# Decoder layer on one core: one transposed copy of h, waits in another order, first tile and gate-weight sum on VectorE

## What is computed

```python
def weight_quant(w):
    scale = 1.0 / jnp.clip(jnp.mean(jnp.abs(w)), 1e-05, None)
    return jnp.clip(jnp.round(w * scale), -1, 1) / scale

def _L0_ffn_ref(x, gate_w, down_w, gate_norm_w, down_norm_w):
    y = bit_linear(x, gate_w, gate_norm_w)
    gate, up = jnp.split(y, 2, axis=-1)
    h = gate * jax.nn.sigmoid(gate) * up
    return bit_linear(h, down_w, down_norm_w)

x = x + _L0_attn_ref(_layernorm(x, axis=-1), L0_attn_W_qkv, L0_attn_W_out)
x = x + _L0_xattn_ref(_layernorm(x, axis=-1), ctx_2048, mask_BxS2_bk0)
x = x + _L0_ffn_ref(_layernorm(x, axis=-1), L0_ffn_gate_w, L0_ffn_down_w, L0_ffn_gate_norm_w, L0_ffn_down_norm_w)
```

## Time and profile before

| | us |
|---|---|
| median of 3 runs | 209.47 |
| lowest and highest | 208.86, 209.68 |
| the profiled execution | 208.5 |
| its span, first to last instruction | 206.5 |
| busy in it: PE, DVE, ACT, POOL | 186.9, 165.7, 152.2, 113.8 |

### The profile page before, as it was taken

One profiled execution on the slowest core, in us unless ns is written; L12 is line 12 of the kernel. 1 busy time (PEld: TensorE's weight loads), 2 busy tenths in 40 slices (PEclk: granted clock), 3 DMA queues, 4 the chain that ended last, 5 costly groups with the idle time before them and its releaser, 6 DMA issues.

```text
span 206.5 us, 10407 instructions
## 1 busy us (share of the span) xinstructions
PE 186.9 (91%) x3967; PEld 149.6 (72%) x3967; DVE 165.7 (80%) x522; ACT 152.2 (74%) x438; POOL 113.8 (55%) x258
## 2 busy tenths in 40 slices
PE   3999999999998999999999999999999998885673
PEld 3878688977786778888787879788878776552341
DVE  1335599998895968988998889797979899999982
ACT  2378985858887686879878797977797877575651
POOL 6410328445746362665465575537483558787880
PEclk9999999999999999999999999999999999999999
DMA  5999100101002100020203000202001020300002
GB/s 169 383 342 354 58 3 3 54 3 52 3 0 86 51 3 25 0 78 2 76 0 103 28 29 2 76 2 73 3 26 52 20 63 27 103 5 2 25 25 76
DMA packets 11474, 12.82 MB, mean 62 GB/s; under 512 B 1010, under 2 KB 10674, under 8 KB 11444
## 3 DMA queue, kind: packets, MB, share of 16 engines
q1 hardware_dynamic: 11444, 12.46, 18.6%
HBM read 10.36 MB, written 2.10 MB: 60 GB/s over the span
## 4 chain that ended last, share of the span: by engine, by line
PE 73%; issue 8%; DVE 7%; ACT 7%; POOL 2%; DMA 1%; ACTq 1%; DVEq 0%; SPq 0%; POOLq 0%
PE ps L366 13%; PE ps L350 8%; PE ps L344 8%; PE ps L376 7%; PE ps L451 5%; PE ps L429 5%; PE ps L533 5%; PE ps L466 5%; PE ps L491 5%; PE ps L398 4%; PE ps L479 3%; PE ps L420 2%; PE ps L388 2%; PE ps L550 2%; DVE wg L1411 1%
## 5 line engine op out<-in xcount | busy, mean ns | idle before, releaser
L2006 POOL TENSOR_TENSOR zh<-hh,gd 128x352 f32<-128x352 f32 x32 | 29.9, 949 | 9.9 <-DVE hh L1350 9.6
L366 PE MATMUL ps<-yaT,wqk 128*128 128x128 f32 x256 | 31.9, 278 | 0.6 <-ACT yaT L701 0.5
L1925 POOL TENSOR_SCALAR ve<-mv 128x1 f32<-128x1 f32 x32 | 7.8, 243 | 42.9 <-issue 34.4
L366 PEld LDWEIGHTS ps<-yaT,wqk 128*128 128x128 f32 x256 | 30.2, 194 | 1.6 <-ACT yaT L701 1.2
L1222 DVE TENSOR_REDUCE mx<-ps 128x16 f32<-128x1024 f32 x16 | 19.6, 1224 | 10.2 <-PE ps L398 9.9
L350 PE MATMUL ps<-wg,zT 128*128 128x352 bf16 x128 | 22.7, 312 | 2.9 <-ACT hT L704 1.3
L805 ACT ACTIVATE th_sb<-ps,th 128x352 f32<-128x352 f32 x32 | 17.5, 552 | 6.5 <-PE ps L350 3.1
L1927 POOL TENSOR_TENSOR rs<-ve,neghalf 128x1 f32<-128x1 f32 x32 | 20.5, 641 | 2.7
L762 ACT ACTIVATE pT<-ps 128x512 f32<-128x512 f32 x32 | 17.8, 597 | 4.4 <-PE ps L436 4.3
L701 ACT ACTIVATE v<-ps 64x128 f32<-64x128 f32 x64 | 17.6, 274 | 2.8 <-PE ps L376 2.2
L350 PEld LDWEIGHTS ps<-wg,zT 128*128 128x128 bf16 x128 | 11.3, 97 | 9.9 <-issue 2.3
(11 more groups left out here) (117 smaller groups left out, 486.6 us busy)
## 6 DMA issues: line engine op xcount, KB each, us to landing
ct_in<-ctx_t SPq DMA_DIRECT2D x16, 128.0 KB, 2.2
cn_in<-ctx_n SPq DMA_DIRECT2D x16, 128.0 KB, 2.2
out<-o_out SPq DMA_DIRECT2D x16, 128.0 KB, 1.7
wg<-gate_t SPq DMA_DIRECT2D x1, 1408.0 KB, 8.2
x_in<-x SPq DMA_DIRECT2D x1, 1024.0 KB, 11.5
wd<-down_t SPq DMA_DIRECT2D x1, 640.0 KB, 8.9
wqk<-wqkv_t SPq DMA_DIRECT2D x1, 512.0 KB, 4.0
x_in<-x SPq DMA_DIRECT2D x1, 512.0 KB, 9.0
```

The source lines that it names most:

```text
L366: last = pe.matmul(qk_ps[:, e * P:(e + 1) * P], wqk[:, c, e * P:(e + 1) * P], yaT[:, t % 2, c, :], start=(c == 0), stop=(c == DC - 1))
L2006: G.tensor_tensor(zh[:, t % 2, part], hh[:, t % 2, part], gd[:, part], ALU.mult).then_inc(ev[f"zh_d{j}"], 1)
```

## The change

- h is transposed in one step of six chunks into bank 0 (`transpose_h`), and one ACT step copies all of it (`keep_hT`). The semaphores hT_ps0/1 and hT_d0/1 become one each.
- In PE's helpers the waits for a free buffer come first and the wait for the data last.
- The first tile is normalised by DVE (`normalise_first`, with the mean and rs1), and POOL leaves out two small operations for it.
- |gate weight| is summed by DVE (`sum_gate`); gate and down weight have each their own total, mean and scale (`total_gate`, `scale_gate`, `total_down`, `scale_down`).
- At the start PE runs 3 matmuls of 512 columns on zeros in hq, after a memset on DVE, in place of 7 of 128 columns on the identity, after its DMA. `keep_busy` has 19 matmuls in place of 15, at other places.
- The lists of all engines are written in another order.

```diff
-WARM = 7
+WARM = 3
...
-        hT_ps = [bank(0, 2 * P).bitcast(F16), bank(5, (IC - 4) * P // 2).bitcast(F16)]
+        hT_ps = bank(0, IC * P // 2).bitcast(F16)
...
             def transpose_ya(t, *users):
-                pe.wait_ge(ev["ya_d"], at(t + 1))
                 freed(users)
+                if isinstance(t, int) and t == 0:
+                    pe.wait_ge(ya_first, 1)
+                else:
+                    pe.wait_ge(ev["ya_d"], at(t))
...
-            def transpose_h_0(t, *users):
+            def transpose_h(t, *users):
                 if first(t):
                     pe.wait_ge(pads_set, 3)
+                freed(users)
                 pe.wait_ge(ev["hq_d"], at(t + 1))
+                transposes(hT_ps, hq_halves[:, t % 2, :, 0], IC, ev["hT_ps"], ident_16)
...
-            def weight_totals(*users):
+            def total(j, wabs, wtot, users):
                 pe.wait_ge(ones_set, 1)
-                pe.wait_ge(wabs, 2)
                 freed(users)
+                pe.wait_ge(wabs, 1)
+                pe.matmul(wtot_ps[:, j:j + 1], ones[:, :], wsum[:, j:j + 1], start=True, stop=True).then_inc(wtot, 1)
...
+            still = hq[:, 0, 0:P]
+            pe.wait_ge(still_set, 1)
+            for _ in range(WARM):
+                pe.matmul(ps[:, 7, :].rearrange("p (n k) -> p n k", k=P), still, still.unsqueeze(1).broadcast_to([P, 4, P]), start=True, stop=True)
             pe.wait_ge(cst_in, 16)
-            for _ in range(WARM):
-                pe.matmul(ps[:, 7, 0:P], ident, ident, start=True, stop=True)
...
-            scores_k(1, ("mT_d", 2))
+            scores_k(1, ("mT_d", 2), ("wmean_g", 1))
...
-                scores_k(s, ("hT_d1", s - 4), ("hh_d0", s - 3), ("hh_d1", s - 3), ("mT_d", s + 1))
-                down(s - 5, ("k0_d", s + 2), ("k1_d", s + 2))
+                transpose_h(s - 5)
+                scores_k(s, ("mT_d", s + 1), ("hh_d1", s - 3), ("hh_d0", s - 3))
+                down(s - 5)
...
-            gate_up_1(15, ("hT_d1", 14))
+            gate_up_1(15, ("hh_d1", 15))
...
-            def sum_gate():
-                act.wait_ge(wg_in, 16)
-                nc.scalar.activation(wg_flat, wg32[:, :], ACT.Abs, accum_out=wsum[:, 0:1]).then_inc(wabs, 1)
...
+            def normalise_first():
+                dve.wait_ge(rstd1[0], 1)
+                V.tensor_scalar(ya[:, 0, :], x_in[:, 0, :], mv1[:, 0, 0:1], rs1[:, 0:1], ALU.subtract, ALU.mult).then_inc(ya_first, 1)
+
+            def sum_gate():
+                dve.wait_ge(wg_in, 16)
+                V.tensor_reduce(out=wsum[:, 0:1], in_=wg32[:, :], op=ALU.add, axis=AX, apply_absolute_value=True).then_inc(wabs_g, 1)
```

More of the change, by code:

```diff
@@ L560, in _ @@
             project_v(1)
-            readout(0)
+            readout(0, ("k1_d", 2))
             scores_q(1)
-            project_qk(2, ("oN_d", 1))
+            transpose_readout(0)
+            project_qk(2)
             transpose_max(1)
-            transpose_readout(0)
-            scores_k(1, ("mT_d", 2))
+            total_gate()
             project_out(0)
-            scores_q(2, ("exp_d0", 2))
+            scores_k(1, ("mT_d", 2), ("wmean_g", 1))
+            transpose_ya(3)
+            project_v(2)
+            scores_q(2, ("exp_d1", 2))
+            transpose_yx(0, ("yaT_d", 4))
             readout(1)
-            project_v(2)
-            transpose_ya(3)
-            weight_totals(("mx_d", 3))
+            transpose_ya(4)
+            cross_scores(0)
             transpose_max(2)
@@ L575, in _ @@
             project_qk(3)
-            transpose_yx(0)
-            scores_k(2, ("wmean_set", 1))
+            scores_k(2, ("mT_d", 3))
             project_out(1)
-            cross_scores(0)
-            transpose_ya(4)
-            scores_q(3, ("exp_d1", 3))
+            total_down(("exp_d1", 3))
             readout(2)
+            scores_q(3, ("wmean_d", 1))
             transpose_cross_weights(0, ("x1_d", 2))
@@ L607, in _ @@
             cross_scores(2)
-            scores_k(4, ("hh_d0", 1))
-            transpose_cross_weights(2, ("x1_d", 4))
+            scores_k(4, ("hh_d1", 1))
+            transpose_cross_weights(2)
             project_v(5)
@@ L639, in _ @@
             scores_q(15, ("exp_d1", 15))
+            cross_readout(12)
             transpose_z(11)
             readout(14)
-            cross_readout(12)
-            gate_up_0(11, ("mx_d", 16))
             transpose_yx(13)
-            gate_up_1(11)
+            gate_up_1(11, ("mx_d", 16))
+            gate_up_0(11)
+            cross_scores(13)
             transpose_readout(14)
-            cross_scores(13)
-            transpose_h_0(10)
+            transpose_h(10)
             project_out(14)
             transpose_max(15, ("h1_d0", 12))
-            transpose_h_1(10, ("h1_d1", 12))
             down(10)
             transpose_cross_weights(13, ("x1_d", 15))
-            scores_k(15, ("hh_d1", 12), ("mT_d", 16))
+            scores_k(15, ("hh_d0", 12))
             cross_readout(13)
@@ L1524, in _ @@
             scale_rz(2)
-            residual_1(4)
             scale_qz(2)
-            cross_sums_inverse(3)
-            stats_x1(4)
-            round_z(2)
-            residual_3(0)
-            inner_largest(1)
-            variance_x1(4)
-            scale_hm(1)
-            maxima(6)
+            stats_x1(4)
+            variance_x1(4)
+            residual_3(0)
+            round_z(2)
+            inner_largest(1)
+            maxima(6)
+            cross_sums_inverse(3)
+            weight_sums_inverse(5)
@@ L1621, in _ @@
-            round_z(5)
             inner_largest(4)
+            maxima(9)
+            cross_sums_inverse(6)
+            max_rest(9)
             cross_guard(6)
-            maxima(9)
+            scale_hm(4)
+            weight_sums_inverse(8)
             residual_2(6)
-            weight_sums_inverse(8)
-            scale_hm(4)
+            normalise_readout(8)
+            gated_0(5)
             scale_rhm(4)
-            normalise_readout(8)
+            inner_0(5)
+            scale_qh(4)
@@ L1703, in _ @@
             scale_zm(8)
-            residual_1(10)
+            variance_x1(10)
             scale_rz(8)
             scale_qz(8)
-            stats_x1(10)
+            round_z(8)
+            residual_3(6)
+            inner_largest(7)
+            maxima(12)
             cross_sums_inverse(9)
-            residual_3(6)
-            round_z(8)
-            variance_x1(10)
-            inner_largest(7)
+            max_rest(12)
+            weight_sums_inverse(11)
             cross_guard(9)
-            maxima(12)
@@ L2065, in _ @@
             rstd_x_4()
+            set_mask(2)
             rstd_x1(1)
```

1032 lines of the change are left out of this document (503 added, 529 removed).

## The result

| | before | after |
|---|---|---|
| median of 4 executions each, us | 209.17 (208.74 to 209.68) | 215.07 (212.77 to 219.70) |
| ratio, 95% interval | | 1.0227 (1.0144 to 1.0311) |
| span of the profiled execution, us | 206.5 | 217.9 |

Slower by 5.9 us; 208.4 was predicted, 210.6 was the end of the range.

What follows compares the result with a forecast made beforehand. PE's own work was taken to bound the kernel from about 6.5 to 165 us, then DVE's list for 40 us. Terms 0.3 - 0.9 - 0.4 - 0.1 = -1.1 took the median from 209.5 to 208.4, range 206.6 to 210.6.

Steps and rivals of the forecast that it cites:

- Start: Until project_qk(0) ends: PE fast earlier, gain of 0.6 us at 9.8, 0.35 carried, bounds 0.2 to 2.0.
- The sum on DVE: Gate weight's sum before 17.71 on DVE: 3.1 us in idle time, ends about 16.6, costs nothing.
- Tiles 0 to 4: Head up to the loop's start: new order 0.3 us later in sum, bounds -1.5 to +1.5.
- The +0.9: Head, once cross scores 0 and output projection 1 are done: the new order is 0.9 us late.
- the 0.6 "regained": Later in the head: gate weight rounded before z(0)'s rush, fewer PE waits, 0.6 us won back.
- nothing regained: Rival: the head's 0.9 us lateness stays and the loop gives nothing, 209.9 us; chance 0.24.
- The loop: 8 steps from 77.26 to 164.32: 0.9 of PE's 1.4 us waits at L420 before scores_k goes.
- The single copy: ACT's one copy of h, 768 columns in 0.88 us, just in time for down, nothing to spare.
- The slower rival: Rival: ACT copies h late, down waits 0.35 us in each of 10 steps, 211.9 us; chance 0.12.
- The end: Behind the maxima of tile 15: DVE fed sooner, -0.4 us, between -1 and +0.6.
- The sum 0.3 - 0.9 - 0.4 - 0.1: Whole kernel: loop's start +0.3, loop -0.9, end -0.4, wait order -0.1, together -1.1 us.
- the wait of 1.8 us: Head: PE stands still 1.8 us before transpose_yx(0), from 25.15 until ACT's copy is ready at 26.9.

Runs made afterwards that it cites:

- oneh: Kernel before with only the single transposed copy of h (one ACT copy, no wait for it in scores_k): 209.53 against 209.35 us, ratio 0.9995.
- start_same: Kernel before with the new start alone, its start matmuls as 2 wide and 5 of 128 columns, keeping 28 entries: 209.34 us, ratio 1.0004.
- yaT_first: Changed kernel with one swap on ACT, keep_yaT(3) ahead of normalise_x1(0): 215.28 us (212.37 to 218.06).
- both_pad20: Changed kernel with 12 start matmuls of 128 columns, 9 unread matmuls before transpose_yx(0), 10 unread one-column start matmuls: 207.66 us, ratio 0.9924.
- start_wide: Kernel before with the new start alone, three start matmuls of 4 x 128 columns (12 entries): 214.59 us, ratio 1.0175.

## Why the prediction was wrong, step by step

- **Start: right in its rows, but its gain is not shown.** First matmul at 1.04; `project_qk(0)` 6.89 with 2.02 and done at 8.9 (1.95 and 9.2 were said). The start matmuls took 4.5 us and not 5.5, and the first tile on DVE became what PE waits for, by 0.31. `project_qk(1)` starts at 11.32 against 11.68, the 0.35 that I carried. But I had read one execution of the old start: `oneh`, which has the same start as before, has `project_qk(0)` at 7.08 with 2.05 and `project_qk(1)` at 11.01, earlier than after. The agreement is luck, and `start_same` measured no gain. (I also put the first transposes of before at 6.53; the row has 6.32.)
- **The sum on DVE: right.** 3.08 us at 13.05 for 3.1 at 13.2, and DVE still waits 1.40 behind it.
- **Tiles 0 to 4: right in kind, 0.6 short.** PE waits 2.19 (2.07 in the other execution) for 1.8; the last link is not ACT's yx but the copy of ya(3) queued behind it, which `yaT_first` moved (1.7). In the execution with a full clock `scores_q(5)` is at 56.84; without the 2.29 of the late fetch that would be 54.55, and 53.9 was said. The +0.9 stayed, and the 0.6 "regained" was not seen: the rival "nothing regained" describes the head.
- **The loop: wrong.** 8 settled steps take 87.06 us before and, in both_pad20, 86.85 (76.48 to 163.33): 0.2 for 0.9. PE's waits in these steps, in before (77.26 to 164.32) and then in both_pad20:

```profile
PE ps L420 <- ACT kz L734: 0.6, 2, 0.4
PE ps L420 <- issue: 0.4, 2, 0.3
```

```profile
PE ps L345 <- DVE hq L1365: 0.7, 1, 0.7
```

  So the 1.4 us were 1.0 (the fifth wait, at 74.12, lies ahead of these steps), and a new wait for DVE's hq before `transpose_h` takes 0.7 of it back. What the loop gained is in its first two steps, 21.4 against 23.7 us, where before has the stops of 0.96 and 0.37 us at entries 2184 and 2434: the kernel before pays for late instructions too. In after that gain goes into its stop of 2.05 and the clock behind it.
- **The single copy: right.** 0.811 us for 0.88, no wait of `down` in the loop. The slower rival stayed away.
- **The end: wrong sign.** -0.4 was said; +0.6 in both_pad20 and +2.1 to +2.2 in after. `cross_scores(14)` now stands ahead of `project_out(15)` and waits for the context's DMA (1.38, 1.17, 0.55 us), and in the other execution of after the clock is at 0.57 from 186 to 190. I had compared DVE's list, which is the same, and not asked what its feeder waits for. (`keep_busy` has 21 matmuls after, not 19.)
- **The step that failed** is the account of what bounds the kernel: "It can gain only at the start, where PE stands still between 6.5 and 165, and at what DVE waits for at the end." The sum 0.3 - 0.9 - 0.4 - 0.1 has terms for work and for semaphores and none for the place of instructions in PE's list, which was put at nothing without a reason. In its place the runs showed stops of 2.29 and 2.05 us at entries 440 and 2682, and the clock at 0.50 behind them and behind the wait for yx(0). The page of before had the hint, in its row of `project_v`:

```profile
L376 PE MATMUL ps<-wv,yaT 128*128 128x256 f32 x64 | 16.9, 385 | 1.0 <-issue 1.0
```

  And "the granted clock reads 1.00 (2.4 GHz) in that stretch as everywhere" was true of before, but I took it over for after, where it fell to 0.50 behind three stops: the wait of 1.8 us was priced at 1.8, and in one trace of two it cost more. Both together cost 5.2 us in `start_wide`, which has only the start of the change, and 7.4 us between after and both_pad20, which has all of it.
- With these out of the way the kernel is 1.6 us faster than before (0.0076 of 209.55; the two traces differ by 0.4). That it is near the 1.1 of the sum is luck: in the traces the terms are -2.5 in the loop, +1.5 in the head, +0.6 at the end. It isn't the worth of the change alone either, since before keeps its own late instructions, 0.96 + 0.37 us. Before with its list shifted so that these go was not run; it may be as fast.

## What to carry to other kernels

Before a sum of moved work is trusted, look for stops "ended by nothing" on PE, in the trace of before too, count at which entry of PE's list they come, and shift the list by a few unread one-column matmuls: a change that costs 5 us can be that alone. Do the same to the kernel before, or the comparison is not fair. Price a wait of 2 us on PE at up to twice its length, since the clock may be at half behind it (4.6 us for two such waits between the two traces of after), and try matmuls that nobody reads in it; they shift the list too, so look at both. Time such a kernel often enough to see whether it has two groups of times.
